# Self attention's amplitudes and phases loaded and weighed in cross attention's tail; fold factors in eighths into four places

## The chip, the cores and the metric

The kernel runs on one core of a Trainium2 chip. It has five engines that run side by side and meet through semaphores: TensorE (PE in the profile, with its weight loads as PEld), VectorE (DVE), ScalarE (ACT), GpSimd (POOL) and SyncE (SP), which here issues most DMAs. The metric is the device time of one execution in microseconds. Before the change it is 1698.99 us (median of 3 runs, 1696.46 to 1701.09).

## The reference

One block of a Perceiver-like network, on x (64 x 32 x 512) and a context of 64 x 257 x 128. The part that matters here is in its order:

1. Cross attention of 32 query rows per batch over 257 context rows, 16 heads, with rotary embedding of queries and keys, and its output added to x (call it x1).
2. Layer norm of x1, then self attention within each batch (32 rows, 16 heads of 32). Each of its four linear maps is given by a basis (64 x 512), and a weight `w = amp * cos(phase)`; a map is `(x @ basis.T) @ w.T`. Its output is added to x1 (x2).
3. Layer norm of x2, then a feed-forward part. A gate makes h = sqrt(2) cos(pi tanh(x @ ph_w + ph_b) - pi/4) * sigmoid(x @ amp_w + amp_b). Then there are two layers. The first half of a layer is h + (h @ ent_w + ent_b) @ ent_pw + ent_pb, with ent_w 512 x 2048 and ent_pw 2048 x 512; the second is h plus the sum of two path maps times a modulation. Each half ends in a layer norm. No nonlinearity stands between ent_w and ent_pw, so the kernel multiplies the two matrices with each other once ("folds" them), and adds the identity.

## The kernel before

The kernel is a series of blocks, and at the end of each all engines wait for each other: `query_path`, `cross_attention`, `root_deviations`, `holo_weights`, `self_attention`, `root_deviations`, `fold_weights`, `feed_forward`. Within a block each engine has its own program in order, and waits on semaphores.

`cross_attention` (L670 to L1018) handles 16 tiles of 128 rows (4 batches each), software pipelined. Tile t is projected (`project`, 48 matmuls, written as three products of rounded high and low parts) while later tiles are scored. The last batch's `add_end` (L842, VectorE) needs weights of the last context row that SyncE has stored to memory and read back spread over all partitions (`spread_ends`, L742 and L744). After it come ScalarE's `round_mixed` (L913) and GpSimd's `split_mixed` (L794), and only then `project` of tile 15. After the loop VectorE does `add_end`, and `add_out` and `keep_moments` for tiles 14 and 15.

`holo_weights` (L1049 to L1129) forms self attention's weights. SyncE issues six loads (phases, amplitudes, the output basis, and `basis`), VectorE waits for all six, reduces the phases (1280 columns) to within half a turn in four steps (L1079 to L1082), ScalarE takes |.| and a sine (L1100, L1102), VectorE multiplies by the amplitudes (L1088). TensorE then makes 32 small products (L1120, L1126), from which VectorE copies `score_w` (L1092) and ScalarE `value_w` (L1107). `self_attention` (L1132 to L1408) starts afterwards: GpSimd clears `e_t` and `keys` and normalises the first rows, TensorE transposes them (`turn_input`), and multiplies them with `basis` (`reduce_input`, L1223). At its start SyncE issues the first loads of the fold (`FoldLoads.first`), which land during self attention.

`fold_weights` (L1440 to L1617) handles two layers. The factors of a layer, `left` (ent_in) and `right` (ent_out), are 16 slices k of 512 columns each, and come in four quarters of 4 slices (1 MB of each factor) into two places. TensorE multiplies (L1518), VectorE forms the bias through the fold with one step per slice (`sum_entangled`, L1559 and L1560). SyncE loads a quarter into a place when TensorE has used the one that was there and VectorE has accumulated it:

```
                for q in range(QUARTERS):
                    turn = QUARTERS * l + q
                    if turn >= 2:
                        sp.wait_ge(quarter_used, turn - 1)
                        sp.wait_ge(accumulated, (turn - 1) * KQ)
                        loads.quarter(sp, l, q)
```

VectorE's program in this block is: wait for a broadcast load of 12 rows (`rows_loaded`), form the modulation (L1596 to L1603), copy `out_norm`, `sum_entangled(0)`, `finish` of the entangling and of the path matrix of layer 0, `sum_entangled(1)`, the biases, `finish` for layer 1. GpSimd multiplies the path matrices by the modulation (L1496) and adds them (L1500), once VectorE has formed it. Layer 1's products start when ScalarE has copied layer 0's out of PSUM.

## Time and profile before

| | |
|---|---|
| median of 3 runs | 1698.99 us |
| time of the profiled execution | 1701.08 us |
| its span, first to last instruction | 1699.3 us |
| mean granted TensorE clock | 0.947 |
| TensorE matmuls busy | 1490.1 us (88%) |
| VectorE busy | 1126.8 us (66%) |
| ScalarE busy | 809.9 us (48%) |
| GpSimd busy | 540.8 us (32%) |
| holo_weights, first DMA issue to the first of self_attention | 988.87 to 1011.30 us |
| fold_weights, first matmul to the last product of the factors | 1189.28 to 1329.01 us |

Times in the timeline are from the start of the span. A row of it names the engine, the line of the kernel, what is written from what, and in brackets how long the engine was idle before and who released it. The granted clock is given as a share of full speed: 1.00 is 2.4 GHz, 0.50 is 1.2 GHz.

### The profile page before, as it was taken

What the parts mean: (1) busy time and instruction counts of PE and PEld (TensorE: products, weight loads), DVE (VectorE), ACT (ScalarE), POOL (GpSimd) and SP (SyncE); (2) the same over time, 40 slices, a digit from 0 to 9 for tenths busy, and PEclk for the clock granted to TensorE, in tenths of its full rate; (3) what the DMA queues carried; (4) which work ended last, traced back from release to release, by engine and by line L of the source; (5) the groups of instructions that cost most, each with busy time, mean ns of one, the idle gap of its engine ahead of it and who ended that gap; (6) DMA issues with size and microseconds to landing.
All of it is one profiled execution on the core that took longest, in us unless ns stands there. A gap on an engine that the chain in (4) does not pass through costs nothing. (4 is left out here: it accounts for less than half of the span.)

```text
span 1699.3 us, 26369 instructions
## 1 busy us (share of the span) xinstructions
PE 1490.1 (88%) x8136; PEld 1129.8 (66%) x8136; DVE 1126.8 (66%) x1816; ACT 809.9 (48%) x1723; POOL 540.8 (32%) x594
## 2 busy tenths in 40 slices
PE   5799999999758999999999929997689499999996
PEld 3577777777546777777777728886234277777775
DVE  6788877887346877877887625775628626464746
ACT  4556656556434555555555414554100344545553
POOL 4234433331034455455445312120321311312202
PEclk9899999999978999999999969998889699999998
DMA  4132333432366444454444122000253000000000
GB/s 155 54 106 85 115 99 106 124 105 87 91 205 197 121 118 115 108 124 109 108 123 114 43 103 93 0 0 1 84 237 149 0 1 1 26 1 25 1 25 25
DMA packets 138010, 143.77 MB, mean 85 GB/s; under 512 B 83169, under 2 KB 102753, under 8 KB 134241
## 3 DMA queue, kind: packets, MB, share of 16 engines
q1 hardware_dynamic: 136224, 133.86, 27.0%
q10 hardware_dynamic: 1728, 9.20, 1.6%
q8 instruction: 29, 0.48, 0.1%
q14 instruction: 29, 0.23, 0.1%
HBM read 113.54 MB, written 29.49 MB: 84 GB/s over the span
## 5 line engine op out<-in xcount | busy, mean ns | idle before, releaser
L901 ACT ACTIVATE c_e_t_high<-c_et_ps 128x512 fp32r<-128x512 f32 x128 | 76.7, 599 | 227.1 <-PE c_et_ps L966 227.1
L794 POOL TENSOR_TENSOR c_mixed_low<-c_whole,c_mixed_high 128x512 fp32r<-128x512 f32 x64 | 95.3, 1489 | 174.8 <-ACT c_mixed_high L913 174.8
L77 DVE TENSOR_TENSOR b_rot_parts_low<-b_rot,b_rot_parts_high 128x1536 fp32r<-128x1536 f32 x64 | 135.8, 2122 | 21.8 <-ACT b_rot_parts_high L526 21.8
L958 PE MATMUL c_sc_ps<-c_kv_t,c_q 128*128 128x257 f32 x512 | 136.3, 390 | 15.1 <-DMA c_q<-carried_queries 15.1
L1518 PE MATMUL f_ps<-f_right,f_left 128*128 128x512 f32 x256 | 115.3, 612 | 27.7 <-DMA f_right<-ent_out 20.4
L817 DVE TENSOR_REDUCE c_peak<-c_sc_ps 128x2 f32<-128x514 f32 x128 | 88.5, 692 | 56.7 <-PE c_sc_ps L958 56.0
L264 POOL TENSOR_TENSOR b_turned_raw<-b_turn_part 128x384 f32<-128x384 f32 x32 | 70.0, 2188 | 167.6 <-DVE b_key_parts_low L77 166.3
L70 PE MATMUL e_mm_ps<-folded_high,e_h_t_high 128*128 128x512 f32 x256 | 108.8, 425 | 15.8 <-DVE e_h_t_low L77 15.6
L958 PEld LDWEIGHTS c_sc_ps<-c_kv_t,c_q 128*128 128x128 f32 x512 | 99.1, 195 | 34.2 <-DMA c_q<-carried_queries 15.9
L309 DVE TENSOR_TENSOR b_rot<-b_w_qr,b_angle 128x1536 f32<-128x1536 f32 x64 | 119.1, 1861 | 0.2
L893 ACT ACTIVATE c_e<-c_sc_ps,c_peak 128x257 f32<-128x257 f32 x256 | 118.8, 475 | 0.0
L966 PE MATMUL c_et_ps<-ident,c_e 128*128 128x128 f32 x512 | 83.1, 286 | 34.9 <-DVE c_e L824 32.4
L70 PE MATMUL b_ps<-b_x_t_high,b_wq_parts_high 128*128 128x512 f32 x256 | 107.4, 419 | 6.7 <-DVE b_x_t_low L77 6.7
L1518 PEld LDWEIGHTS f_ps<-f_right,f_left 128*128 128x128 f32 x256 | 49.9, 197 | 93.1 <-issue 65.2
L70 PE MATMUL c_out_ps<-c_w_vo_high,c_mixed_high 128*128 128x512 f32 x256 | 110.7, 433 | 1.2 <-POOL c_mixed_low L794 1.2
L77 DVE TENSOR_TENSOR c_e_t_low<-c_et_ps,c_e_t_high 128x512 fp32r<-128x512 f32 x128 | 87.9, 687 | 30.9 <-ACT c_e_t_high L901 30.9
L526 ACT ACTIVATE b_rot_parts_high<-b_rot 128x1536 fp32r<-128x1536 f32 x64 | 95.3, 1489 | 24.5 <-PE b_ps L72 17.0
L1702 POOL TENSOR_TENSOR e_y<-e_y,out_norm 128x512 f32<-128x512 f32 x16 | 22.5, 1406 | 263.1 <-DVE e_y L1862 263.1
L966 PEld LDWEIGHTS c_et_ps<-ident,c_e 128*128 128x128 f32 x512 | 60.5, 145 | 68.7 <-DVE c_e L824 62.1
L260 POOL TENSOR_TENSOR b_turn_part<-b_early,b_centre 128x384 f32<-128x384 f32 x64 | 82.1, 1304 | 72.0 <-DMA b_early<-early 70.3
L71 PE MATMUL e_mm_ps<-folded_low,e_h_t_high 128*128 128x512 f32 x256 | 103.5, 404 | 0.0
L72 PE MATMUL e_mm_ps<-folded_high,e_h_t_low 128*128 128x512 f32 x256 | 103.3, 404 | 0.0
(212 smaller groups left out, 3956.5 us busy)
## 6 DMA issues: line engine op xcount, KB each, us to landing
c_q<-carried_queries SPq DMA_DIRECT2D x64, 256.0 KB, 3.7
c_ends_spread<-end_weights SPq DMA_DIRECT2D x64, 256.0 KB, 4.3
carried_queries<-x SPq DMA_DIRECT2D x7, 2048.0 KB, 11.2
b_early<-early SPq DMA_DIRECT2D x15, 640.0 KB, 4.0
c_raw<-cache_t SPq DMA_DIRECT2D x64, 128.5 KB, 3.9
c_swapped<-cache_t SPq DMA_DIRECT2D x128, 64.2 KB, 3.9
f_left<-ent_in SPq DMA_DIRECT2D x8, 1024.0 KB, 5.3
f_right<-ent_out SPq DMA_DIRECT2D x8, 1024.0 KB, 8.0
```

The lines of the kernel that those rows point to most:

```text
L70: nc.tensor.matmul(out, left[0], right[0], start=start, stop=False)
L71: nc.tensor.matmul(out, left[0], right[1], start=False, stop=False)
L72: return nc.tensor.matmul(out, left[1], right[0], start=False, stop=stop)
L77: return nc.vector.tensor_tensor(low, value, high.bitcast(F32), ALU.subtract)
L309: nc.vector.tensor_tensor(rot[:, k % 2], weight, angles, ALU.mult).then_inc(rot_ready, 1)
L526: nc.scalar.activation(rot_parts[0][:, k % 2], rot[:, k % 2], ACT.Copy).then_inc(rot_rounded, 1)
L794: nc.gpsimd.tensor_tensor(mixed[1][:, w, :, u], whole[:, u % 2].rearrange("p (h s) -> p h s", h=H), mixed[0][:, w, :, u].bitcast(F32), ALU ...
L817: nc.vector.tensor_reduce(peak[:, v], sc_ps[:, 2 * v:2 * v + 2, 0:L], AX_X, ALU.max, negate=True).then_inc(peaked, 1)
L893: last = nc.scalar.activation(e[:, v, c], sc_ps[:, 2 * v + c, 0:L], ACT.Exp, bias=peak[:, v, c:c + 1], accum_out=total[:, v, c:c + 1])
L958: last = nc.tensor.matmul(sc_ps[:, 2 * half + c, 0:L], q[:, u, at], kv_t[:, u], start=True, stop=True)
L966: last = nc.tensor.transpose(et_ps[:, (2 * k + c) * P:(2 * k + c + 1) * P], e[:, half, c, k * P:(k + 1) * P], ident[:])
L1518: last = nc.tensor.matmul(ps[:, m], left[:, slot, m * P:(m + 1) * P], right[:, slot], start=k == 0, stop=k == CF - 1)
```

## The change

The block `holo_weights` is gone. Two areas, phases and amplitudes, lie in a tile `spare` that lives through the whole kernel, and that `query_path`, `fold_weights` and `feed_forward` use for some of their own tiles (`b_p`, `b_qr`, `f_acc`, `f_ones`, `e_y`, `e_scratch` and small ones).

- SyncE issues five loads (all but `basis`) in `cross_attention`, after the loads of the last tile and ahead of that tile's four `spread_ends`.
- VectorE does the four steps on the phases after its last `split_turned` and ahead of the last `add_end`; its turns lie in `c_q`. It multiplies by the amplitudes after `keep_moments` of tile 14. ScalarE does |.| and sine after its last `round_mixed`.
- `self_attention` issues `basis` first, and begins with the 32 small products, the values first. ScalarE copies `value_w` and VectorE `score_w` ahead of their programs; TensorE waits for `value_w` before `turn_input`, for `basis` before `reduce_input` and for `score_w` before the steps. `out_w` is no longer copied, but read where it lies.
- In the fold a layer's factors come in eight pieces of 2 slices (0.5 MB of each factor) into four places; the places hold as much as before. The bias's first eight steps go ahead of VectorE's wait for `rows_loaded`. `out_norm` is loaded by a DMA of its own, not copied.

```diff
+    def load(self, sp, loaded):
+        nat = HOLO - D
+        sp.dma_start(self.phase[:, 0:nat], self.phase_nat.rearrange("p t i -> p (t i)")).then_inc(loaded, 16)
+        sp.dma_start(self.phase[:, nat:], self.phase_o).then_inc(loaded, 16)
+        sp.dma_start(self.amp[:, 0:nat], self.amp_nat.rearrange("p t i -> p (t i)")).then_inc(loaded, 16)
+        sp.dma_start(self.amp[:, nat:], self.amp_o).then_inc(loaded, 16)
+        sp.dma_start(self.basis_out, self.basis_o).then_inc(loaded, 16)
...
             in_tiles(sp, tile)
+            holo.load(sp, holo_loaded)
             for u in range(BT):
                 spread_ends(TILES - 1, u)
...
             in_tiles(dve, tile)
+            phase, turns = holo.phase, q[:].rearrange("p u x -> p (u x)")[:, 0:HOLO]
+            dve.wait_ge(holo_loaded, 80)
+            dve.wait_ge(scored, 2 * B)
+            nc.vector.tensor_scalar(turns, phase, 1.0 / (2 * PI), MAGIC, ALU.mult, ALU.add).then_inc(holo_stepped, 1)
+            dve.wait_ge(holo_stepped, 1)
+            nc.vector.tensor_scalar(turns, turns, MAGIC, None, ALU.subtract).then_inc(holo_stepped, 1)
+            dve.wait_ge(holo_stepped, 2)
+            nc.vector.scalar_tensor_tensor(phase, turns, -TURN_HI, phase, ALU.mult, ALU.add).then_inc(holo_stepped, 1)
+            dve.wait_ge(holo_stepped, 3)
+            nc.vector.scalar_tensor_tensor(phase, turns, -TURN_LO, phase, ALU.mult, ALU.add).then_inc(holo_stepped, 1)
             add_end(TILES - 1, BT - 1)
-            for t in (TILES - 2, TILES - 1):
-                add_out(t)
-                keep_moments(t)
+            add_out(TILES - 2)
+            keep_moments(TILES - 2)
+            dve.wait_ge(holo_cosined, 2)
+            nc.vector.tensor_tensor(holo.amp, holo.amp, phase, ALU.mult).then_inc(holo_weighed, 1)
+            add_out(TILES - 1)
+            keep_moments(TILES - 1)
...
             round_mixed(B - 1, BT - 1, TILES - 1, 1)
+            act.wait_ge(holo_stepped, 4)
+            nc.scalar.activation(holo.phase, holo.phase, ACT.Abs).then_inc(holo_cosined, 1)
+            act.wait_ge(holo_cosined, 1)
+            nc.scalar.activation(holo.phase, holo.phase, ACT.Sin, bias=half_pi[:], scale=-1.0).then_inc(holo_cosined, 1)
...
         @block.sync
         def _(sp):
+            sp.dma_start(basis[:], basis_t).then_inc(basis_loaded, 16)
             loads.first(sp)
...
+            last.then_inc(weights_done, 1)
+            pe.wait_ge(value_w_out, 8)
             turn_input(0, 0)
+            pe.wait_ge(basis_loaded, 16)
             reduce_input(0, 0)
+            pe.wait_ge(score_w_out, 1)
             in_steps(pe, step)
...
-LAYERS, PW, QUARTERS = 2, 2, 4
-KQ = CF // QUARTERS
+LAYERS, PW, PIECES, SLOTS = 2, 2, 8, 4
+KQ = CF // PIECES
...
-                for q in range(QUARTERS):
-                    turn = QUARTERS * l + q
-                    if turn >= 2:
-                        sp.wait_ge(quarter_used, turn - 1)
-                        sp.wait_ge(accumulated, (turn - 1) * KQ)
-                        loads.quarter(sp, l, q)
+                for q in range(PIECES):
+                    turn = PIECES * l + q
+                    if turn >= SLOTS:
+                        sp.wait_ge(piece_used, turn - SLOTS + 1)
+                        sp.wait_ge(accumulated, (turn - SLOTS + 1) * KQ)
+                        loads.piece(sp, l, q)
...
+            dve.wait_ge(loads.col_loaded, 16)
+            sum_entangled(0, range(SLOTS * KQ))
             dve.wait_ge(rows_loaded, 16)
...
-            nc.vector.tensor_copy(out_norm[:], row[:, NR - 2:NR])
-            sum_entangled(0)
+            sum_entangled(0, range(SLOTS * KQ, CF))
             finish(0, 0)
             finish(1, 1)
-            sum_entangled(1)
+            sum_entangled(1, range(CF))
```

## Rows read from the trace of the kernel before

**Rows 1.** Page, part 2: the granted clock of TensorE in 40 slices.

```profile
PEclk9899999999978999999999969998889699999998
```

**Rows 2.** Timeline, cross to self attention: start, us, engine, line, what [idle before <-releaser].

```profile
988.87 0.34 SPq L1067 DMA_DIRECT2D h_phase<-phase_nat  x1
...
997.39 0.83 DVE L1079 TENSOR_SCALAR h_turns<-h_phase 128x1280 f32<-128x1280 f32 x1 [9.01 <-DMA basis<-basis_t]
...
1000.64 1.49 DVE L1082 SCALAR_TENSOR_TENSOR h_phase<-h_turns,h_phase 128x1280 f32<-128x1280 f32 x1
...
1007.76 0.81 PE L1120 MATMUL h_ps<-h_amp 32*64 32x64 f32 x20 [23.64 <-DVE h_amp L1088]
...
1009.62 1.44 ACT L1107 ACTIVATE value_w<-h_ps 64x128 f32<-64x128 f32 x8 [3.52 <-PE h_ps L1126]
...
1011.30 0.33 SPq L1434 DMA_DIRECT2D f_col<-columns  x1
...
1017.62 3.78 PE L1223 MATMUL d_ps<-d_xn_t,basis 128*128 128x128 f32 x16 [0.75 <-ACT d_xn_t L1358]
```

**Rows 3.** Timeline, end of cross attention: VectorE, GpSimd, TensorE.

```profile
965.50 0.69 DVE L77 TENSOR_TENSOR c_e_t_low<-c_et_ps,c_e_t_high 128x512 fp32r<-128x512 f32 x1 [0.33 <-ACT c_e_t_high L901]
969.75 1.13 DVE L842 SCALAR_TENSOR_TENSOR c_whole<-c_ends_spread,c_kv_t,c_mix_ps 128x512 f32<-128x512 f32 x1 [3.56 <-DMA c_ends_spread<-end_weights]
...
966.07 1.29 POOL L794 TENSOR_TENSOR c_mixed_low<-c_whole,c_mixed_high 128x512 fp32r<-128x512 f32 x1 [1.68 <-ACT c_mixed_high L913]
971.63 1.26 POOL L794 TENSOR_TENSOR c_mixed_low<-c_whole,c_mixed_high 128x512 fp32r<-128x512 f32 x1 [4.27 <-ACT c_mixed_high L913]
...
972.95 0.50 PE L70 MATMUL c_out_ps<-c_w_vo_high,c_mixed_high 128*128 128x512 f32 x1 [1.19 <-POOL c_mixed_low L794]
```

**Rows 4.** Timeline, fold_weights: VectorE, GpSimd, queue of SyncE.

```profile
1214.02 4.74 DVE L1559 TENSOR_SCALAR f_acc<-f_right,f_col 128x512 f32<-128x512 f32 x1
...
1286.77 0.48 DVE L1559 TENSOR_SCALAR f_acc<-f_right,f_col 128x512 f32<-128x512 f32 x1
1287.29 9.60 DVE L1560 SCALAR_TENSOR_TENSOR f_acc<-f_right,f_col,f_acc 128x512 f32<-128x512 f32 x7
...
1213.46 9.66 POOL L1496 TENSOR_TENSOR paths<-paths,f_row 128x2048 f32<-128x2048 f32 x2 [24.24 <-DVE f_row L1603]
...
1293.82 0.33 SPq L1430 DMA_DIRECT2D f_left<-ent_in  x1
```

**Rows 5.** Timeline, last tile of cross attention: queue of SyncE, VectorE.

```profile
943.64 0.33 SPq L744 DMA_DIRECT2D c_ends_spread<-end_weights  x1
...
950.31 1.12 DVE L842 SCALAR_TENSOR_TENSOR c_whole<-c_ends_spread,c_kv_t,c_mix_ps 128x512 f32<-128x512 f32 x1
```

**Rows 6.** DMA issues: KB each, median us from issue to landing.

```profile
c_ends_spread<-end_weights SPq DMA_DIRECT2D x64, 256.0 KB, 4.3
...
f_left<-ent_in SPq DMA_DIRECT2D x8, 1024.0 KB, 5.3
...
basis<-basis_t SPq DMA_DIRECT2D x1, 512.0 KB, 6.2
...
h_bo<-basis_o SPq DMA_DIRECT2D x1, 128.0 KB, 5.0
```

**Rows 7.** Timeline, fold_weights: TensorE.

```profile
1189.28 29.92 PE L1518 MATMUL f_ps<-f_right,f_left 128*128 128x512 f32 x64 [4.95 <-POOL f_ones L1490]
1237.00 29.95 PE L1518 MATMUL f_ps<-f_right,f_left 128*128 128x512 f32 x64 [17.81 <-DMA f_right<-ent_out]
1269.26 27.70 PE L1518 MATMUL f_ps<-f_right,f_left 128*128 128x512 f32 x64 [2.31 <-ACT f_raw L1537]
1296.80 1.88 PE L1507 MATMUL f_bias_ps<-f_acc,f_ones 128*128 128x512 f32 x4
1301.28 27.73 PE L1518 MATMUL f_ps<-f_right,f_left 128*128 128x512 f32 x64 [2.60 <-DMA f_right<-ent_out]
```

**Rows 8.** Window: length, PE, PEld, DVE, ACT, POOL busy, clock, DMA, GB/s.

```profile
1016.00:1026.00 10.00, 8.44 (x41) 7.52 (x40) 0.00 (x0) 1.90 (x5) 3.77 (x4) 0.50 1.02 408
```

More of the change, by code:

```diff
@@ L1131, in self_attention @@
-def self_attention(nc, x1, stat, basis, score_w, value_w, out_w, ident, loads):
+def self_attention(nc, x1, stat, holo, basis_t, ident, loads):
     with ExitStack() as ctx:
@@ L1290, in step, with rows @@
                     project(t - 1)
+            weights = holo.amp[:, 0:NAT].rearrange("p (t w i) -> p t w i", t=CD, w=3)
+            def rows(h):
+                return slice(h % 4 * HD, h % 4 * HD + HD), h // 4
+            for hh in range(HH):
+                h, c, k = head_of(hh), hh // 8, hh % 4 // 2
+                at, t = rows(h)
+                last = nc.tensor.matmul(ps[HARM:2 * HARM, VALUE_BANKS[h % 4], (2 * c + k) * HARM:(2 * c + k + 1) * HARM], weights[at, t, 2],
+                                        holo.basis_out[at, t], start=True, stop=True)
+            last.then_inc(weights_done, 1)
+            for h in range(HH):
+                at, t = rows(h)
+                last = nc.tensor.matmul(ps[0:HARM, SCORE_BANKS[h % 4], t * HARM:(t + 1) * HARM], weights[at, t, 0], weights[at, t, 1],
+                                        start=True, stop=True)
+            last.then_inc(weights_done, 1)
+            pe.wait_ge(value_w_out, 8)
             turn_input(0, 0)
+            pe.wait_ge(basis_loaded, 16)
             reduce_input(0, 0)
+            pe.wait_ge(score_w_out, 1)
             in_steps(pe, step)
@@ L1631, in load, with feed_forward @@
         sp.dma_start(self.bias[:], self.gate_b).then_inc(self.loaded, 16)
-def feed_forward(nc, x2, stat, gate, folded, bias, out_norm, eps, half_pi, ident, out):
+def feed_forward(nc, x2, stat, gate, spare, folded, bias, out_norm, eps, half_pi, ident, out):
     with ExitStack() as ctx:
@@ L1645, in feed_forward @@
         T = G * P
-        y = sb("e_y", [P, G, D])
+        y = spare[:, 0:G * D].rearrange("p (u d) -> p u d", u=G)
         weights = pair("e_weights", [P, 2, CD, D])
@@ L1941, in perceiver_block @@
             loads = FoldLoads(nc, fold_scope, paths, ent_in, ent_out, path, columns)
-            with ExitStack() as scope:
-                basis, score_w, value_w, out_w = (scope.enter_context(nc.sbuf_tensor(n, shape, F32)) for n, shape in (
-                    ("basis", [P, CD, 2 * P]), ("score_w", [HARM, 16, HARM]), ("value_w", [P, 16, HARM]), ("out_w", [P, D])))
-                holo_weights(nc, amp_nat, phase_nat, basis_t, basis_o, amp_o, phase_o, half_pi, basis, score_w, value_w, out_w)
-                self_attention(nc, x1, stat, basis, score_w, value_w, out_w, ident, loads)
+            self_attention(nc, x1, stat, holo, basis_t, ident, loads)
             root_deviations(nc, stat, eps, "x2")
-            fold_weights(nc, loads, path, rows, half_pi, ident, folded, bias, out_norm, gate)
-        feed_forward(nc, x1, stat, gate, folded, bias, out_norm, eps, half_pi, ident, out)
+            fold_weights(nc, loads, path, rows, spare, half_pi, ident, folded, bias, out_norm, gate)
+        feed_forward(nc, x1, stat, gate, spare, folded, bias, out_norm, eps, half_pi, ident, out)
 def rope_tables(length, dim):
```

198 lines of the change are left out of this document (78 added, 120 removed).

## The prediction, made before the result was known

> **What bounds the kernel now.** I read the page first: TensorE is by far the busiest engine, and its granted clock is lowest in slices 23 and 31 (counted from 0), and a little low in 27 to 29 [rows 1]. A slice is 42.5 us, so these are the way from cross to self attention (about 984 to 1016 us) and the fold with what is behind it (1189 to 1345 us). The change touches just these, so next come the timelines there. Between blocks all engines meet, so time taken off a block's longest chain moves everything behind it.
>
> From cross to self attention TensorE idles 23.64 us until the amplitudes are weighed [rows 2]. The reader should see a chain without any overlap: SyncE issues at 988.87, VectorE waits until 997.39 for the last of six loads, four steps, ScalarE, the multiplication, the small products, ScalarE's copies until 1011.06, and only at 1011.30 does self attention begin [rows 2].
>
> In the fold TensorE needs 27.70 us for half a layer. The first two halves took 29.92 and 29.95 us, each behind idle time, and between them it waited 17.81 us for a load; in layer 1 it waited 2.60 us for another [rows 7]. The first of these loads went out late because VectorE reached its bias steps late: they begin at 1214.02, behind the modulation, and the first takes 4.74 us against 0.48 us in layer 1 [rows 4].
>
> **Step 1, the block of the weights goes.** Self attention's first DMA issue moves from 1011.30 to where holo_weights' was, 988.87, relative to the end of cross attention: -22.43 us [rows 2]. One pair of barriers goes with it, and is in that number.
>
> **Step 2, what comes into self attention's start.** The 32 small products (64 matmuls in the trace) ran from 1007.76 to about 1009.6, the value copies until 1011.06: 3.3 us from start to end [rows 2]. With T for the new block's start they are done at T+3.5. Before the change TensorE needed nothing of this sort before it reached `reduce_input` at 1017.62, T+6.32, held by GpSimd's clearing and normalising and then by a transpose. Those are unchanged, and TensorE's transposes wait for GpSimd to about T+4.4. So the products are hidden by GpSimd: 0, and without that cover 3.3 us. `basis` is issued first at T; it landed 6.2 us after its issue with five loads ahead of it [rows 6], and even so it would be there at T+6.2, before T+6.32: 0. The other issues that SyncE has here, one for the columns, eight for the pieces and one for the paths, feed nothing before the fold.
>
> **Step 3, what comes into cross attention's tail.** The last `split_turned` ends at 965.50 + 0.69 = 966.19. Before, VectorE then idled 3.56 us for the spread weights and did `add_end` at 969.75 [rows 3]. Now four steps stand between. Two take 0.83 us, two 1.49 us, with their gaps 4.74 us (997.39 to 1000.64 + 1.49 = 1002.13) [rows 2]. Alone this would end at 970.95, 1.2 us late. But GpSimd works on `c_mixed_low` from 966.07 to 967.36 [rows 3], and in the fold a VectorE step of 0.48 us took 4.74 us beside a GpSimd product of 9.66 / 2 = 4.83 us that had begun 0.56 us before it [rows 4]: it waited for that product to end. I take the same here: the first step begins only at 967.36, and the last ends at 972.1. `add_end` is 2.4 us late. Nobody absorbs that: `round_mixed`, `split_mixed` (971.63) and TensorE's project of tile 15 (972.95, after 1.19 us idle) follow directly [rows 3]. +2.4 us, with ends 1.2 and 4 (if the DMA of the spread is late too, below).
>
> The other new work is hidden. ScalarE's |.|, table load and sine take some 4 us from about 974; they and then `square_row` of tile 14 and the multiplication of 1.49 us lie beside the 48 matmuls of tile 15, which last 11 us (972.95 to 1007.76 - 23.64 = 984.12) [rows 2, 3]. The table load only moves. SyncE issues the five loads while it would wait for GpSimd's end weights of the last tile, whose spread went out at 943.64 and its store 1.4 us before that [rows 5]; their bytes are the next point.
>
> **Step 4, the five loads' bytes.** They are 1.4 MB. If the last goes out at 940.8 (an estimate: five issues from 938.6) and lands 5.0 us later, as that of the output basis did [rows 6], the queue is free at 945.8. The store of the end weights then finishes about 2 us late, and so does the spread behind it. Before, the spread landed at 943.64 + 4.3 = 947.9, and the `add_end` that needs it began at 950.31 without waiting [rows 5, 6]: 2.4 us to spare. So 0, up to +2.
>
> **Step 5, the fold.** Four pieces are in place at the start, just what the two quarters were. VectorE's first eight steps now go before the rows land: they read what is there and GpSimd does nothing, so they end by about 1196. So piece 5 waits only for TensorE's use of piece 1 (about 1199) and is there some 6 us later; TensorE wants it at 1219.2. In steady state a place is refilled while three others are multiplied, 3 x 6.9 = 20.8 us (27.70 / 4 each), and a load needs 5.3 us per MB [rows 6]. So the wait of 17.81 us goes, and with it the slow beginning of the second half, 29.95 - 27.70 = 2.25 us [rows 7].
>
> What is late next is layer 1. Its fifth piece waits for two bias steps, and VectorE comes to those only after both `finish`. In the times of before, the load that waited for four of them went out at 1293.82 [rows 4]; with two fewer, of some 0.7 us each ((9.60 - 4.8) / 7, with one of the seven held up by GpSimd for the rest), at 1292.4. Two transfers of 0.5 MB are the bytes of one `f_left`, 5.3 us [rows 6]: landed at 1297.7. TensorE finishes the first half and two bias products at 1296.80 + 1.88 = 1298.68 [rows 7]. So the 2.60 us go as well, with 1.0 us to spare. The 2.31 us for ScalarE's copy stay. The second layer's later pieces have more room, the path load of layer 1 lands beside products, and `out_norm` is needed only in the feed-forward part. Sum: -(17.81 + 2.25 + 2.60) = -22.66 us. Bounds: -17.8, if the clock's loss came elsewhere and the last wait stayed, and -22.7.
>
> The row of loads says 5.3 us for 1 MB, at 408 GB/s while the first pieces land [rows 6, 8]. The Trainium skill, "DMA: Bandwidth & Descriptors", section "Measured (HBM→SBUF, 128 partitions, SWDGE, issued from GpSimd)", speaks against this part: it advises transfers of at least 1 MiB, and the pieces are half of that. An estimate by that page's fit (2.0 us plus the bytes at 436 GB/s, two in a row) is 6.4 us for a pair, 0.1 us too late for layer 1's fifth piece: the sum would change by 0.1 us.
>
> **Sum.** -22.43 + 2.4 - 22.66 = -42.7 us. The profiled execution took 1701.08 us (span 1699.3, and 1.8 around it), which gives 1658.4. It lay 2.1 us over the median of 1698.99; taken from the median the result is 1656.3 us.
>
> **Rivals.**
> A. The forecast: 1656.3, with its own range of 1653 to 1660. Chance 0.60.
> B. TensorE's clock is still up when self attention begins, since its idle time is now about 5 us in place of 23.64 [rows 2]. In the ten microseconds from 1016 it was at 0.50 with 8.44 us busy [rows 8]; at full speed that is 4.2 us less: 1652.1. Against it: besides 2 us of small products it idles almost all of T to T+4.4. Chance 0.12.
> C. The five loads delay the spreads, or VectorE's steps block more than I count, up to 4 us more: 1660. The slack of 2.4 us against a delay of 2 is thin. Chance 0.12.
> D. Layer 1's fifth piece is late again, by up to the old 2.60 us, and later ones with it: 1659 to 1662. The slack is 1.0 us. Chance 0.10.
> E. The fold's half does not do what it says: piece loads wait for VectorE as before, because its first eight steps are held by something, and only the weights' part stays: 1656.3 + 22.7 = 1679. The program's order speaks against it. Chance 0.04.
> F. Slower than before: small pieces. If a pair of 0.5 MB took longer than the 6.9 us TensorE needs for it, all 12 refilled pieces would be waited for; from 10.5 us for a pair (12 x 3.6 = 43) it eats the whole gain, at 11 us it costs 49 us: 1705. That is 95 GB/s, against 408 in the row [rows 8]. Chance 0.02.
>
> Together the range that holds 8 in 10 is 1651 to 1663. 0.3% (5 us) is about what a measurement of this kernel can tell from no change. Faster by more than that: A to E, 0.97; within: 0.01; slower: 0.02.
>
> **What would show it.** Step 1: no idle of 23 us before the small products, but about 5. Step 2: `reduce_input` at T+6.3, waiting for ScalarE and not for `basis`. Step 3: the first phase step begins after GpSimd's `c_mixed_low` or reads 2 us; project of tile 15 starts 2.4 us later than the last `split_turned` would have it. Step 5: layer 0's products in one run of about 57.6 us, and only ScalarE's 2.3 us between the layers. The prediction is wrong if TensorE shows a wait for `f_right` beyond 1 us, or a wait for `basis`.

## The result and the profile after

The changed kernel takes 1657.74 us (median of 4 runs, 1656.85 to 1663.18), the kernel before 1699.70 us beside it (4 runs, 1696.46 to 1701.09). The two medians differ by 42.0 us (quotient 0.9753); the ratio that weighs all the runs is 0.9762, with a 95% interval of 0.9737 to 0.9788. Forecast were 1656.3 us, in a range of 1651 to 1663. The profiled execution has a span of 1655.7 us (time 1657.46) against 1699.3 before, so 43.6 us are to be found.

The table cuts both spans at places that each execution has: SyncE's first issue in self attention, its first issue in the fold, and TensorE's first and last product of the factors. The last row takes in the 0.28 and 0.27 us between the fold's first issue and its first product.

| stretch, us | before | after | difference |
|---|---|---|---|
| start to self attention's first issue | 1011.30 | 992.37 | -18.93 |
| self attention, to the fold's first issue | 177.70 | 176.78 | -0.92 |
| fold, first to last product of the factors | 139.73 | 116.47 | -23.26 |
| the rest of the span | 370.57 | 370.08 | -0.49 |

In the page of the kernel after, the row of granted clocks (40 slices, now of 41.4 us) reads as follows. The 6 that stood on the way from cross to self attention [rows 1] has become a 9 and an 8 (slices 23 and 24), and slices 27 and 29 have risen from 8 to 9. Slice 29 (1200 to 1242 us) lies in the fold and has no wait for a load any more. Slice 27 says nothing of the fold: before the change it ended at 1189 us, where the fold began, and since the slices are now shorter it holds another part of self attention. The 6 of slice 31, at the end of the fold and behind it, has stayed.

```profile
PEclk9899999999968999999999998999899699999998
```

**The tail of cross attention.** First the timeline of the kernel after for VectorE, GpSimd and TensorE, where the phase steps were put (start, duration, engine, line, what, idle time before and who ended it). It answers to [rows 3].

```profile
965.27 0.69 DVE L77 TENSOR_TENSOR c_e_t_low<-c_et_ps,c_e_t_high 128x512 fp32r<-128x512 f32 x1 [0.32 <-ACT c_e_t_high L942]
965.87 1.93 DVE L911 TENSOR_SCALAR c_q<-spare 128x1280 f32<-128x1280 f32 x1
967.84 0.83 DVE L913 TENSOR_SCALAR c_q<-c_q 128x1280 f32<-128x1280 f32 x1
...
970.23 1.49 DVE L917 SCALAR_TENSOR_TENSOR spare<-c_q,spare 128x1280 f32<-128x1280 f32 x1
971.64 1.11 DVE L868 SCALAR_TENSOR_TENSOR c_whole<-c_ends_spread,c_kv_t,c_mix_ps 128x512 f32<-128x512 f32 x1
...
965.83 1.29 POOL L820 TENSOR_TENSOR c_mixed_low<-c_whole,c_mixed_high 128x512 fp32r<-128x512 f32 x1 [1.68 <-ACT c_mixed_high L954]
973.48 1.27 POOL L820 TENSOR_TENSOR c_mixed_low<-c_whole,c_mixed_high 128x512 fp32r<-128x512 f32 x1 [6.36 <-ACT c_mixed_high L954]
...
974.80 0.50 PE L70 MATMUL c_out_ps<-c_w_vo_high,c_mixed_high 128*128 128x512 f32 x1 [3.33 <-POOL c_mixed_low L820]
```

The first of two equal steps reads 1.93 us and the second 0.83 us: GpSimd was at work on `c_mixed_low` until 967.12, and the first step ends 0.68 us behind that. `add_end` (L868) starts 6.37 us after the last `split_turned`, where it took 4.25 us before [rows 3]: 2.12 us late. TensorE's project of tile 15 starts after 3.33 us of idle time instead of 1.19. What comes next stood in no term of the forecast. The windows of the kernel after for this stretch (bounds, length, busy time of PE, PEld, DVE, ACT, POOL, granted clock, DMA share, GB/s):

```profile
974.00:975.00 1.00, 0.20 (x1) 0.20 (x2) 0.00 (x0) 0.98 (x2) 0.75 (x1) 1.00 0.06 16
975.00:976.00 1.00, 1.00 (x4) 0.76 (x4) 0.00 (x0) 0.99 (x2) 0.00 (x0) 0.82 0.00 0
976.00:977.00 1.00, 1.00 (x4) 0.80 (x3) 0.00 (x0) 1.00 (x1) 0.00 (x0) 0.50 0.00 0
...
979.00:980.00 1.00, 1.00 (x6) 0.82 (x5) 0.59 (x1) 0.00 (x0) 0.00 (x0) 0.97 0.00 0
```

TensorE begins at 974.80 at a clock of 1.00; from about 975.6 to 979.1 the clock is at 0.50 (1.2 GHz), and tile 15's 48 products take 12.83 us (974.80 to 987.63) instead of 11.17. The stretch's -18.93 us are thus -22.43 (the block that went) + 2.12 (`add_end`) + 1.66 (the clock) - 0.28 (at the last `split_turned` this execution was 0.23 us ahead of the one before, and 0.05 are left over).

**The start of self attention.** Timeline of the kernel after, queue of SyncE, TensorE and ScalarE, which answers to [rows 2]:

```profile
992.37 0.33 SPq L1157 DMA_DIRECT2D d_basis<-basis_t  x1
...
992.41 0.67 PE L1265 MATMUL d_ps<-spare 32*64 32x64 f32 x21 [4.78 <-PEq L1070]
...
996.91 1.08 PE L1180 MATMUL d_ps<-ident,d_xn 128*128 128x128 f32 x4 [2.95 <-POOL d_xn L1171]
998.84 3.75 PE L1188 MATMUL d_ps<-d_xn_t,d_basis 128*128 128x128 f32 x16 [0.84 <-ACT d_xn_t L1346]
...
994.00 1.44 ACT L1394 ACTIVATE d_value_w<-d_ps 64x128 f32<-64x128 f32 x8 [2.40 <-PE d_ps L1270]
```

The idle time before the small products is 4.78 us instead of 23.64. The transposes wait for GpSimd (2.95 us), not for `value_w`, and `reduce_input` waits for ScalarE at T+6.47, not for `basis`.

**The fold.** Timeline of the kernel after, TensorE and VectorE, which answers to [rows 7] and [rows 4]:

```profile
1169.42 57.27 PE L1515 MATMUL f_ps<-f_right,f_left 128*128 128x512 f32 x128 [4.96 <-POOL spare L1487]
1229.00 27.70 PE L1515 MATMUL f_ps<-f_right,f_left 128*128 128x512 f32 x64 [2.31 <-ACT f_raw L1534]
1256.55 1.88 PE L1504 MATMUL f_bias_ps<-spare 128*128 128x512 f32 x4
1258.26 27.63 PE L1515 MATMUL f_ps<-f_right,f_left 128*128 128x512 f32 x64
...
1169.29 0.49 DVE L1556 TENSOR_SCALAR spare<-f_right,f_col 128x512 f32<-128x512 f32 x1 [0.61 <-PEq L1070]
1169.81 5.48 DVE L1557 SCALAR_TENSOR_TENSOR spare<-f_right,f_col,spare 128x512 f32<-128x512 f32 x7
```

Layer 0 is one run of 57.27 us, from the first product to the last 20.40 us shorter than before (77.67: 1189.28 to 1237.00 + 29.95). Layer 1, from its first product to its last, takes 56.89 us instead of 59.75, 2.86 us less. The 2.31 us between the layers are the same. VectorE's first step takes 0.49 us instead of 4.74; GpSimd has no product beside it now.

### The profile page after: what moved, and what is told of

It is laid out like the page before. It is cut to its first block and busy times, and to the rows that moved or that the text cites. A ratio compares the mean times of both kernels' runs of the same rounds, so it can differ in the third digit from the quotient of the medians.

```text
span 1655.7 us, 26391 instructions
## 1 busy us (share of the span) xinstructions
PE 1485.7 (90%) x8136; PEld 1127.4 (68%) x8136; DVE 1126.5 (68%) x1814; ACT 810.0 (49%) x1723; POOL 541.2 (33%) x594
## 5 line engine op out<-in xcount | busy, mean ns | idle before, releaser
L1700 POOL TENSOR_TENSOR spare<-spare,out_norm 128x512 f32<-128x512 f32 x16 | 22.4, 1401 | 262.7 <-DVE spare L1860 262.7
L1828 ACT ACTIVATE spare<-spare 128x512 f32<-128x512 f32 x64 | 46.4, 725 | 118.7 <-DVE spare L1853 118.7
```

## The experiments

Each kernel is the changed one with the edit shown, except where it says otherwise; the kernel before ran beside each. Ratios are to it. Dummy products write places in PSUM that nobody reads. In weights_only, quarters and sixteenths one more line, not shown, keeps layer 0's two bias products at the middle of layer 1, where they are in the changed kernel (`if l and q == PIECES // 2 - 1`).

| kernel | median, us (lowest to highest, runs) | ratio [95%] | span of its profile |
|---|---|---|---|
| weights_only | 1681.19 (1680.29 to 1683.01, 4) | 0.9895 [0.9877, 0.9913] | 1678.5 |
| quarters | 1660.86 (1658.93 to 1663.32, 5) | 0.9772 [0.9755, 0.9788] | 1661.2 |
| late_sums | 1673.55 (1669.57 to 1675.33, 4) | 0.9842 [0.9821, 0.9863] | 1671.8 |
| sixteenths | 1656.05 (1654.66 to 1658.22, 5) | 0.9744 [0.9728, 0.9759] | 1652.9 |
| basis_last | 1670.30 (1669.66 to 1671.38, 4) | 0.9824 [0.9806, 0.9841] | 1668.3 |
| steps_behind | 1655.42 (1652.09 to 1657.31, 5) | 0.9732 [0.9715, 0.9748] | 1655.5 |
| fill | 1657.74 (1656.95 to 1662.36, 5) | 0.9756 [0.9738, 0.9774] | 1655.9 |
| warm | 1651.91 (1650.18 to 1653.17, 5) | 0.9715 [0.9700, 0.9731] | 1650.1 |
| warm_fold | 1654.62 (1651.92 to 1656.95, 5) | 0.9741 [0.9719, 0.9764] | 1650.1 |
| warm_all | 1650.18 (1649.35 to 1656.36, 5) | 0.9717 [0.9693, 0.9741] | 1654.5 |

### weights_only: the fold's part undone

```diff
-LAYERS, PW, PIECES, SLOTS = 2, 2, 8, 4
+LAYERS, PW, PIECES, SLOTS = 2, 2, 4, 2
...
-            dve.wait_ge(loads.col_loaded, 16)
-            sum_entangled(0, range(SLOTS * KQ))
             dve.wait_ge(rows_loaded, 16)
+            dve.wait_ge(loads.col_loaded, 16)
...
-            sum_entangled(0, range(SLOTS * KQ, CF))
+            sum_entangled(0, range(CF))
```

> The changed kernel with the fold's part undone: factors in quarters into two places and all of the bias steps behind the modulation, as before. Theory (the two halves of the change are independent and add up): TensorE's wait of 17.8 us in layer 0 and that of 2.6 us in layer 1 are back, with the slow clock behind the first (2.3 us), so the span is 23 us over the changed kernel's 1655.7: 1679, a time of about 1681. Rival (self attention's share was larger than its row, the fold's smaller): below 1676.

Measured: 1681.19 us, as expected. By its ratio it is 1.05% under the kernel before, 17.8 us (the medians differ by 18.4), and the whole change is 2.38% under it: so by the ratios the two halves are worth 17.8 and about 22.6 us. Its trace has the fold's old picture, TensorE rows of weights_only:

```profile
1168.96 29.67 PE L1515 MATMUL f_ps<-f_right,f_left 128*128 128x512 f32 x64 [4.96 <-POOL spare L1487]
1215.54 30.27 PE L1515 MATMUL f_ps<-f_right,f_left 128*128 128x512 f32 x64 [16.91 <-DMA f_right<-ent_out]
```

and a tail of cross attention like that of the kernel after (27.02 us from the last `split_turned` to self attention, 12.76 us for tile 15's products, against 27.10 and 12.83). The fold takes 138.92 us here and 139.73 in the kernel before, so it is the same with and without the other half; layer 1's wait is 0.98 us instead of 2.60, behind a half that took 29.33 us. So far as these two stretches show it, the halves stand apart. The fold's half alone was not run.

### quarters and late_sums: which part of the fold's edit does it

quarters keeps the early bias steps and goes back to two places of a quarter each; late_sums keeps eighths in four places and puts all bias steps of layer 0 behind the modulation.

```diff
 quarters:
-LAYERS, PW, PIECES, SLOTS = 2, 2, 8, 4
+LAYERS, PW, PIECES, SLOTS = 2, 2, 4, 2
 late_sums:
-            dve.wait_ge(loads.col_loaded, 16)
-            sum_entangled(0, range(SLOTS * KQ))
             dve.wait_ge(rows_loaded, 16)
+            dve.wait_ge(loads.col_loaded, 16)
...
-            sum_entangled(0, range(SLOTS * KQ, CF))
+            sum_entangled(0, range(CF))
```

> The changed kernel with factors in quarters into two places, but the first eight bias steps still ahead of the wait for the rows. Theory (the early bias steps take away layer 0's wait, the eighths only layer 1's): TensorE runs through layer 0 without a wait, because the third quarter's load goes out at TensorE's use of the first quarter, some 16 us after the fold's start, and lands 7.5 us later, before 29.6; in layer 1 it waits 2.6 us again. Span 1658.3, time about 1660.5. Rival (the eighths take away layer 0's wait): a wait of 10 us or more in layer 0, time 1670 or more.

> The changed kernel with eighths into four places, but all bias steps behind the modulation, as before. Theory (the wait in layer 0 comes from the place of the bias steps): the fifth piece's load waits for two of VectorE's steps, which come some 24 us after the fold's start and are held up by GpSimd's products of 4.8 us each, so it goes out at about 34 us and lands at 39 to 40 against 30 when TensorE wants it: a wait of 9 to 10 us and 2.3 us of slow clock, span 1667 to 1668, time 1669 to 1670. Rival (smaller pieces are enough): no wait, 1657.7.

Measured: quarters 1660.86, late_sums 1673.55 us. TensorE in the fold of quarters:

```profile
1168.88 57.31 PE L1515 MATMUL f_ps<-f_right,f_left 128*128 128x512 f32 x128 [4.96 <-POOL spare L1487]
...
1260.50 29.43 PE L1515 MATMUL f_ps<-f_right,f_left 128*128 128x512 f32 x64 [2.57 <-DMA f_right<-ent_out]
```

and in that of late_sums:

```profile
1208.64 30.68 PE L1515 MATMUL f_ps<-f_right,f_left 128*128 128x512 f32 x64 [9.23 <-DMA f_right<-ent_out]
1241.64 29.40 PE L1515 MATMUL f_ps<-f_right,f_left 128*128 128x512 f32 x64 [2.31 <-ACT f_raw L1534]
```

With the early steps alone layer 0 has no wait at all, and the fold takes 121.05 us; only layer 1's wait is left, 2.57 us, with 1.7 us of slow products behind it. With the eighths alone it takes 130.45 us: the load still goes out late (1203.60, when VectorE's two first steps are through, the first of them 4.84 us long beside GpSimd), and the wait of 16.91 us becomes 9.23. With both it is 116.47, with neither 138.92. The early steps alone bring 17.9 of the 22.5 us, the eighths alone 8.5, and they overlap by 3.9. Quarters came out as expected. Late_sums' total was some 4 us above what I had expected, though its wait was as expected: behind both of its idle times the products ran slowly (30.68 and 29.40 us instead of 27.70), where I had counted on one slow stretch of 2.3 us, and the rest of its span behind the fold was 1.8 us longer than in the changed kernel. In medians, quarters and the full change differ by 3.1 us, and their intervals overlap: the eighths' 4.6 us are seen in the stage, not in the total.

### sixteenths: smaller pieces still

```diff
-LAYERS, PW, PIECES, SLOTS = 2, 2, 8, 4
+LAYERS, PW, PIECES, SLOTS = 2, 2, 16, 8
```

> The changed kernel with the fold's factors in sixteen pieces of one slice (0.25 MB of each factor) into eight places. Theory (what counts is that a load goes out early enough; the rate of small pieces is not the bound): no wait for a load in either layer, the fold takes as long as in the changed kernel (116.5 us from the first matmul to the last product), time 1657.7 within 0.2%. Rival (small pieces lose the DMA's rate, as the Trainium skill's page on DMA, Bandwidth and Descriptors, advises at least 1 MiB for a transfer; by the fit in its section on measured rates, an estimate of 5.2 us for a pair in a row, against 3.5 us that TensorE needs): each of the 24 refilled pieces would be waited for by up to 1.7 us, up to 40 us more, 1660 to 1698.

Measured: 1656.05 us, 0.9744, against 0.9762 for eighths: no difference that can be told. The fold takes 116.53 us (116.47). In the page of sixteenths the loads read (count, KB, median us from issue to landing):

```profile
f_left<-ent_in SPq DMA_DIRECT2D x32, 256.0 KB, 4.3
f_right<-ent_out SPq DMA_DIRECT2D x32, 256.0 KB, 5.0
```

and in that of the kernel after:

```profile
f_left<-ent_in SPq DMA_DIRECT2D x16, 512.0 KB, 5.5
f_right<-ent_out SPq DMA_DIRECT2D x16, 512.0 KB, 6.8
```

A load of 256 KB, a quarter of the size before the change, still takes 4.3 us, but it is issued seven places ahead (three with eighths), and the transfers overlap. The rule of the Trainium skill against transfers under 1 MiB ("DMA: Bandwidth & Descriptors", "Measured (HBM→SBUF, 128 partitions, SWDGE, issued from GpSimd)") is one of efficiency. Here, down to 256 KB, it doesn't reach the time, as the kernel wants only a pair of 256 KB in 27.7 / 8 = 3.5 us. The expectation's estimate of 5.2 us for a pair adds up the fit for one load over two (2.0 us plus the bytes each; on that page of the Trainium skill it stands ahead of the section that the expectation names), and no wait came of it: loads in flight together are not to be added up so. Rival F was excluded by the trace of the changed kernel already, and this run excludes it for pieces of half the size.

### basis_last: is the place of one load in the queue what keeps Step 2 at nothing?

```diff
         def _(sp):
-            sp.dma_start(basis[:], basis_t).then_inc(basis_loaded, 16)
             loads.first(sp)
+            sp.dma_start(basis[:], basis_t).then_inc(basis_loaded, 16)
```

> The changed kernel with the load of basis issued after the loads of the fold instead of ahead of them. Theory (SyncE's loads are served in the order of their issue, at some 420 GB/s): 10 loads with 6.3 MB stand ahead of it, it is there some 17 us after the block's start, and TensorE's first product with it comes 17 us in place of 6.5 us after the start: about 10.5 us more, time 1668. Rival (loads in flight share the engines evenly, so that a small load is served soon wherever it stands): basis lands within 8 us of its issue, 2 to 7 us more.

Measured: 1670.30 us, 12.6 us over the changed kernel. TensorE in basis_last:

```profile
1011.56 3.78 PE L1188 MATMUL d_ps<-d_xn_t,d_basis 128*128 128x128 f32 x16 [15.06 <-DMA d_basis<-basis_t]
```

Issued at 995.83, the load landed 15.7 us later, behind eight pieces and the paths, instead of 3.8 us. Self attention took 191.11 us instead of 176.78. So the term of 0 for `basis` hangs on one line's place: the reduction was at T+20.7 instead of T+6.5. I had expected T+17 and 1668 us: the order was right, the load came later still.

### steps_behind: the phase steps off the path

The four steps move behind the last `add_end` and `add_out` of tile 14, into TensorE's 11 us for tile 15; ScalarE squares tile 14's row ahead of |.|.

```diff
             in_tiles(dve, tile)
+            add_end(TILES - 1, BT - 1)
+            add_out(TILES - 2)
             phase, turns = holo.phase, q[:].rearrange("p u x -> p (u x)")[:, 0:HOLO]
...
-            add_end(TILES - 1, BT - 1)
-            add_out(TILES - 2)
             keep_moments(TILES - 2)
```

> The changed kernel with VectorE's four phase steps behind the last add_end and add_out of tile 14 instead of ahead of them, and ScalarE's row of squares of tile 14 ahead of the absolute value and sine. Theory (the tail costs 2.1 us by the late add_end, and 1.6 us more because TensorE idles 3.3 us in place of 1.2 and its clock falls to 0.50 in the projection of tile 15): TensorE idles 1.2 us again, the clock stays at 1.00, the projection of tile 15 takes 11.2 us in place of 12.8, self attention begins 3.7 us earlier after the same start of the tail: span 1652.0, time 1654.0. Rival (the weighing, now later, holds up the last add_out, or the clock falls anyway): 0 to 2 us gained.

Measured: 1655.42 us, 0.9732. VectorE and TensorE in steps_behind:

```profile
972.09 1.12 DVE L868 SCALAR_TENSOR_TENSOR c_whole<-c_ends_spread,c_kv_t,c_mix_ps 128x512 f32<-128x512 f32 x1 [3.55 <-DMA c_ends_spread<-end_weights]
...
974.98 0.92 DVE L913 TENSOR_SCALAR c_q<-spare 128x1280 f32<-128x1280 f32 x1
...
975.27 0.50 PE L70 MATMUL c_out_ps<-c_w_vo_high,c_mixed_high 128*128 128x512 f32 x1 [1.21 <-POOL c_mixed_low L820]
```

The idle time before `add_end` is back at its old 3.55 us, TensorE's at 1.21, tile 15 takes 11.18 us at a clock of 1.00, and the first step reads 0.92 us. From the last `split_turned` to self attention it is 23.33 us instead of 27.10: 3.77 us, just the 2.12 of lateness and the 1.66 of the clock. The whole shows less. The median is 2.3 us lower, which the overlapping intervals can't tell from nothing. The profiled execution has nearly the span of the changed kernel's (1655.5 and 1655.7): it reached the last `split_turned` 2.58 us later (967.85), ahead of the edit's place, and its self attention took 1 us longer (177.75).

### fill: is the clock's fall caused by the idle time?

In the changed kernel 12 dummy products of 512 columns stand between tile 14's and tile 15's.

```diff
+            pe.wait_ge(exped, PAIRS)
+            for _ in range(12):
+                nc.tensor.matmul(sc_ps[:, 0], w_vo[0][:, 0, 0:P], w_vo[0][:, 1], start=True, stop=True)
```

> The changed kernel with 12 matmuls of 512 columns added between the projections of tiles 14 and 15, into a bank that nobody reads any more; their result is not used. They fill 2.8 of the 3.3 us in which TensorE idles there. Theory (the clock fell because TensorE idled, and that made the projection of tile 15 take 12.8 us in place of 11.2): it stays at 1.00, the projection takes 11.2 us again, self attention begins 1.6 us earlier after the last split_turned (25.5 us in place of 27.1); add_end stays 2.1 us late. Time about 1656. Rival (the clock falls for another reason, such as GpSimd's or ScalarE's work beside it): 12.8 us as before, 1657.7 or more.

Measured: tile 15 takes 11.19 us instead of 12.83. TensorE in fill:

```profile
971.26 2.88 PE L1067 MATMUL c_sc_ps<-c_w_vo_high 128*128 128x512 f32 x12
974.75 0.50 PE L70 MATMUL c_out_ps<-c_w_vo_high,c_mixed_high 128*128 128x512 f32 x1 [0.61 <-POOL c_mixed_low L820]
```

So in this stage the theory held: the same late `add_end`, 0.61 us of idle time, no fall. This is one execution, and in quarters the clock stayed up without any dummies; what carries the cause is the count over all traces (last section). But the median is 1657.74, the same as without the dummies: in the profiled execution self attention took 179.08 us (176.78), with these windows:

```profile
994.00:1000.00 6.00, 3.94 (x17) 3.60 (x18) 0.00 (x0) 0.60 (x1) 5.12 (x5) 0.50 0.96 331
1000.00:1005.00 5.00, 4.10 (x24) 3.84 (x23) 0.00 (x0) 1.30 (x4) 0.00 (x0) 0.50 1.05 426
1005.00:1010.00 5.00, 4.31 (x31) 3.85 (x30) 2.08 (x3) 1.46 (x2) 1.12 (x2) 0.83 0.96 410
```

The clock came back only at about 1006.7, T+16 (T = 990.68), near the T+15 of the kernel before, and not at T+10.6 as in the kernel after. In this execution the microseconds won by the clock in one stage were lost by it in the next, which begins behind another idle time of 4.8 us. That the one led to the other is not shown: in quarters, too, tile 15 ran at full clock, and its self attention took 175.76 us.

### warm: both idle times filled

steps_behind, with 10 dummy products behind tile 15's, and five of 256 columns behind the 32 small products.

```diff
+            pe.wait_ge(exped, PAIRS)
+            for _ in range(10):
+                nc.tensor.matmul(sc_ps[:, 0], w_vo[0][:, 0, 0:P], w_vo[0][:, 1], start=True, stop=True)
...
             last.then_inc(weights_done, 1)
+            for _ in range(5):
+                nc.tensor.matmul(ps[HARM:2 * HARM, SCORE_BANKS[0], 256:512], ident[:, 0:HARM], row_of(0)[:, 0:256], start=True, stop=True)
             pe.wait_ge(value_w_out, 8)
```

> The kernel with the phase steps behind the last add_end, and matmuls added whose results are not used: 10 of 512 columns behind the projection of tile 15, and 5 of 256 columns in the parts that TensorE does behind the 32 small products of self attention, while it waits for GpSimd. Theory (self attention's first 11 us run at half clock because TensorE idles between the blocks and at the start): the clock stays at 1.00 to the small products, or rises well before the first transposes, and the first tile takes 2 to 4 us less than the 15 us it needs: span some 3 us below that kernel's, time 1652 to 1653. Rival (the first tile waits for GpSimd, ScalarE and VectorE anyway, so the clock costs little; or the added matmuls push the first transposes back): within 1 us of 1655.4, or slower.

Measured: 1651.91 us, 0.9715. TensorE in warm:

```profile
983.67 2.43 PE L1068 MATMUL c_sc_ps<-c_w_vo_high 128*128 128x512 f32 x10
988.77 0.57 PE L1268 MATMUL d_ps<-spare 32*64 32x64 f32 x21 [2.68 <-PEq L1073]
```

and its windows behind that:

```profile
989.00:993.00 4.00, 3.20 (x74) 2.04 (x65) 1.22 (x1) 1.44 (x8) 3.92 (x4) 1.00 0.76 235
993.00:995.00 2.00, 0.89 (x6) 0.71 (x7) 0.00 (x0) 0.60 (x1) 1.92 (x3) 1.00 0.93 298
995.00:997.00 2.00, 1.76 (x16) 1.57 (x15) 0.00 (x0) 0.20 (x2) 1.81 (x3) 1.00 0.99 385
```

With the clock at 1.00 through the start of self attention the stretch takes 174.55 us, 2.23 less than in the kernel after. This is Rival B, brought about on purpose, and warm is the one kernel here whose interval lies wholly under that of the changed kernel (up to 0.9731, against 0.9737 and more). The gain is less than the 4.2 us that I had given it. One cause is in the trace: the second tile fell back to half clock behind a later idle time (its weighing at 1007.25, 1.06 us an instruction, after 2.40 us of waiting for VectorE). In warm_all (below), where it did not fall, the stretch was shorter still, less what later dummies cost there. That part of the slow products had lain beside GpSimd's work, and so had cost nothing, is likely but not measured apart.

### warm_fold and warm_all: the same before the fold and before the feed-forward part

```diff
 warm_fold (warm, and behind self attention's last step):
+            for _ in range(10):
+                nc.tensor.matmul(ps[:, Z_BANK, 0:2 * P], ident[:], basis[:, 0], start=True, stop=True)
 warm_all (warm_fold, and ahead of the feed-forward part's wait for its weights):
+            for _ in range(8):
+                nc.tensor.matmul(mm_ps[:, 3], ident[:], row_of(0), start=True, stop=True)
             pe.wait_ge(weights_split, 2)
```

> The kernel 'warm' plus ten dummy products of 256 columns at the end of self attention's TensorE program, in the 4.96 us in which TensorE idles between self attention's last product (1158.60) and the fold's first (1163.55) in the trace of 'warm'. There the fold's first microseconds ran at a granted clock of 0.50 (1163 to 1168), and layer 0's 128 products cost 2 us more than at full clock. My theory (idle time of some microseconds ahead of a block lets the clock fall, and dummies in it give that back): the ten take 4.3 us at half clock, end before the barrier's end, the fold's first 128 products take 55.4 instead of 57.3 us, and the whole 1650.0 against 1651.9. Rival: the clock of the tail of self attention is already down (0.53 from 1155 to 1158), idle between small products, so the dummies only lift it at their end or push past the barrier: 1651.9 to 1652.5.

> As 'warm_fold', and eight more dummy products of 512 columns at the start of the feed-forward part, where TensorE idles 12.46 us until GpSimd's rows and the split gate weights are there (transposes at 1303.03 in the trace of 'warm'). Eight take 3.5 us at full and 7 us at half clock, from 1295.6 to 1302.6, so they end before the transposes. My theory: the feed-forward part then starts at full clock and gains up to 1.5 us more, 1648.5 to 1649.0. Rival: the transposes there are followed by a wait for VectorE's split rows in which the clock does not matter, or the dummies' lift is lost in it, and the time is that of 'warm_fold'.

Measured: 1654.62 and 1650.18 us, ratios 0.9741 (0.9719 to 0.9764) and 0.9717 (0.9693 to 0.9741), beside warm's 0.9715 (0.9700 to 0.9731). All three intervals overlap: neither expectation was borne out, and nothing is gained that can be told. The traces say why. TensorE in warm_fold at the start of the fold:

```profile
1156.53 4.48 PE L1285 MATMUL d_ps<-d_basis,ident 128*128 128x256 f32 x20
1163.92 55.20 PE L1522 MATMUL f_ps<-f_right,f_left 128*128 128x512 f32 x128 [2.91 <-POOL spare L1494]
```

and in warm_all:

```profile
1157.98 4.48 PE L1285 MATMUL d_ps<-d_basis,ident 128*128 128x256 f32 x20
1165.37 56.90 PE L1522 MATMUL f_ps<-f_right,f_left 128*128 128x512 f32 x128 [2.91 <-POOL spare L1494]
```

Both have the same dummies and the same 2.91 us of idle time behind them. In warm_fold's execution layer 0 ran at full clock from its first product (55.20 us, 2.2 less than in warm). In warm_all's the clock fell at 1166 all the same, layer 0 gained 0.5 us, and the next half, behind the 2.31 us between the layers, took 29.40 us instead of 27.70.

The dummies themselves cost as much as that gain, for they hold up the end of the block. All engines meet there, and ScalarE's next instruction waits for it; the row in warm, and then in warm_fold:

```profile
1160.91 1.28 ACT L1076 ACT_TABLE_LOAD   x1 [0.54 <-PEq L1098]
1161.27 1.28 ACT L1076 ACT_TABLE_LOAD   x1 [2.81 <-PEq L1098]
```

In warm VectorE's last copies end at 1160.61, and ScalarE goes on 0.3 us later. In warm_fold they end at 1158.71, the dummies only at 1161.01, and ScalarE goes on 0.26 us behind those. The idle time is 2.27 us longer, in warm_all too. This is the second half of the rival in warm_fold's expectation, "push past the barrier", and it ate the 2.2 us. The ten dummies were reckoned at 4.3 us at half clock; they took 4.48 us at a clock of 1.00, and the trace counts 20 instructions for them, where the dummies behind tile 15 are one each (x10 in warm, x12 in fill).

With the same dummies at its start as warm, self attention took 174.55 us in warm, 177.57 in warm_fold and 175.73 in warm_all. Less the 2.27 us these are 174.55, 175.30 and 173.46, against 175.76 to 179.08 in the seven kernels without those dummies (the changed one and its variants, but for basis_last). So the gain at the start of self attention stands in three executions. The rest of the span was 1.9 us longer in warm_fold than in warm (371.78 against 369.92), at a lower clock: it was 0.60 from 1338.3 to 1344.3, against 0.84 in the same place of warm. Nothing in the edit tells why.

In warm_all the eight dummies ahead of the feed-forward part took 9.37 us instead of the 7 that I had worked out (16 instructions in the trace), and the transposes stood 9.2 us behind their start (1307.81 and 1298.60), where in warm it was 7.5 from the block's first instruction (1303.03 and 1295.57). The transposes then ran at full clock, and the first product with the gate's weights came 14.65 us behind the block's start, instead of 15.11: about what the dummies delayed is what they gave. The profiled execution was the slowest of its five. Three of them lie at 1649.4 to 1650.2 us, with a mean granted clock of 0.967, against 0.962 and 0.963 in the two slower ones; where they won it no profile shows. The best kernel here is therefore warm or warm_all, 2.8% under the kernel before, and which of the two stays open.

## Why the prediction was right, point by point

- **Step 1** (-22.43 us): as forecast. Between tile 15's last product and self attention's first issue lie 4.74 us in the kernel after; before, 4.75 us lay between it and the block that is gone, so all of the block is out. weights_only has only this half of the change, and its total fits.
- **Step 2** (0): as forecast, with `reduce_input` at T+6.47 instead of T+6.32, waiting for ScalarE. The transposes ahead of it waited for GpSimd, which is the cover that was forecast, and basis_last shows the price of the one line that could spoil it, 12.6 us. `basis`, with nothing ahead of it, landed in 3.8 us instead of 6.2.
- **Step 3** (+2.4, ends 1.2 and 4): the term was 2.12 us for the late `add_end`, by the mechanism forecast: the first step stood behind GpSimd's 1.29 us. What the step missed is its sequel, 1.66 us of half clock in tile 15. Together 3.8, near the upper end, which I had put there for another reason (a late spread): that it still lay inside is luck. steps_behind takes both away (3.77 us), fill only the second (the stretch is 25.48 us instead of 27.10). That another engine's steps delay TensorE was counted, that the delay lowers its clock was not.
- **Step 4** (0, up to +2): the delay was larger than forecast, and the slack just took it. The last tile's first spread went out 5.4 us after its store instead of 1.4: 4.0 us late, where 2 were forecast. The `add_end` that needed it came after 0.58 us of idle time, which the trace puts down to no wait. The rows of SyncE and VectorE in the kernel after:

```profile
947.01 0.33 SPq L769 DMA_DIRECT2D c_ends_spread<-end_weights  x1
...
950.39 1.13 DVE L868 SCALAR_TENSOR_TENSOR c_whole<-c_ends_spread,c_kv_t,c_mix_ps 128x512 f32<-128x512 f32 x1 [0.58 <-issue]
```

  Around 940 this execution was 0.57 us ahead of the one before, at the last `split_turned` 0.23 (965.27 against 965.50), so the loads cost some 0.3 us.
- **Step 5** (-22.66, bound -22.7): -23.26, a little past its bound. Layer 0 gave 20.40 (forecast 17.81 + 2.25), layer 1 2.86 (forecast 2.60). Its fifth piece was issued at 1251.99 and VectorE, which waits for it too, began on it some 5.1 us later, 1.2 us ahead of TensorE's need at 1258.3: the slack of 1.0 us was about right, and Rival D stayed away. Splitting the step showed that most of it comes from the order of VectorE's steps and not from the size of the pieces; the forecast had given the whole wait to both at once.
- **Rival B** (0.12): a part of it came and went. The clock rose at T+10.6 instead of T+15, the first tile's weighing took 0.59 us an instruction, and the second tile's reduction stood at T+16.3 instead of T+18.0. Then the clock was down again (0.65 from 1012 to 1016), and the whole of self attention ended with -0.92. That is in no term.
- **The sum**: -43.6 in the span against -42.7, and this closeness is in part luck. Step 3 lacked 1.4 us, and four differences that the forecast didn't have make up for it and more: -0.9 in self attention, -0.6 in the fold, -0.5 in the rest of the span and -0.3 ahead of the change. All are small beside the 6.3 us by which the four executions of the changed kernel differ.
- **Rivals C, E and F**: C's late spread did come, by 4.0 us, but the slack took it; its other half, a tail longer than counted, is what happened, by the clock, and not to 1660. E did not come. late_sums shows what it would have been: the load waits for VectorE again, but with eighths the wait is 9.23 us, so E's 1679 was too dear, 1673.55. F is excluded by the changed kernel and by sixteenths.

## What to carry to other kernels

A load that is late is first a question of order: ask which engine frees the place, and whether its work can go before a wait that it doesn't need; cutting the loads finer comes second, and costs nothing as long as they are issued several places ahead. Work that is slipped into an engine's idle time is free only if the instruction behind it wasn't on the path; 2.1 us of delay for TensorE cost 1.7 us more in clock, and in five of six executions that cost came. Move such work one instruction later, behind the one that releases TensorE. Dummy products in idle time mostly held the clock (not in warm_all's fold), but they must end before the other engines reach the end of the block: in warm_fold they didn't, and gave back the 2.2 us that they had won. Each stage shows only its own part, so judge them by the median of the whole.

## What the runs showed of the hardware

- A fall of the clock behind short idle time is not the same in every execution. Ahead of tile 15 TensorE idled 3.28 to 3.34 us in six kernels: in five of them tile 15 then took 12.71 to 13.91 us, in quarters 11.18. With 0.61 to 1.51 us ahead of it (before, steps_behind, fill and the three warm kernels) it took 11.17 to 11.19 in all six. In quarters, the row and a window behind it:

```profile
976.94 0.50 PE L70 MATMUL c_out_ps<-c_w_vo_high,c_mixed_high 128*128 128x512 f32 x1 [3.34 <-POOL c_mixed_low L820]
...
978.00:980.00 2.00, 2.00 (x10) 1.66 (x9) 0.00 (x0) 1.99 (x3) 0.00 (x0) 1.00 0.00 0
```

  Behind the 2.31 us between the layers the next 64 products took 27.70 us in nine kernels, and 29.33, 29.40 and 29.40 in weights_only, late_sums and warm_all. A fall costs 1.7 us here, and up to 3 (30.68 instead of 27.70 in late_sums).
- A step of VectorE beside a GpSimd product lasted until that product had ended: 1.93 us instead of 0.83 with a product of 1.29 us, 4.84 instead of 0.49 in late_sums with one of 4.6. The Trainium skill ("SBUF — State Buffer", "SBUF: two separate sides") calls what the two engines share an exclusive lock that is held for the whole instruction. The trace agrees: the first phase step ended 0.68 us behind GpSimd's product. With GpSimd quiet, seven steps took 5.48 us; eight of the same beside GpSimd's two products (9.43 us) and its sum (4.83 us) took 18.88.
- A load waited for those ahead of it in its queue: the 512 KB of `basis` took 3.8 us at the head of SyncE's queue and 15.7 us behind 6 MB.
